# Grouped attention of a four-block network: each head's scores, transposes and projection products in two halves in place of four quarters

## The reference, cut to what matters

```
def _L1_attn_ref(x, Wq, Wk, Wv, Wo):          # x: 2 x 512 x 512
    q = einsum('bth,oh->bto', x, Wq)          # 32 heads x 128
    k = einsum('bth,oh->bto', x, Wk)          # 8 heads x 128
    v = einsum('bth,oh->bto', x, Wv)          # 8 heads x 128
    q = q * cos + _rotate_half(q) * sin
    k = k * cos + _rotate_half(k) * sin
    qg = q.reshape(B, 8, 4, T, 128)
    scores = einsum('bkgtd,bksd->bkgts', qg, k) / sqrt(128)
    scores = where(causal, scores, -inf)
    attn = softmax(scores, axis=-1)
    out = einsum('bkgts,bksd->bkgtd', attn, v)
    return einsum('bto,ho->bth', out, Wo)
```

## Time and profile before

| | us |
|---|---|
| median of 3 runs | 2234.25 (2228.36 to 2234.79) |
| the profiled execution's own time | 2234.35 |
| its span in the profile | 2232.6 |
| TensorE busy (matrix products) | 2007.4, 90% of the span |
| TensorE weight loads busy | 1263.8, 57% |
| VectorE busy | 1110.2, 50% |
| ScalarE busy | 777.2, 35% |
| GpSimd busy | 742.5, 33% |

### The profile page before, as it was taken

How to read it: one execution, slowest core, us unless ns; L and a number is a source line. 1 busy time by engine, 2 the same in 40 slices (tenths; PEclk the granted TensorE clock), 3 DMA queues, 4 the chain that set the end, 5 groups by cost and what they waited for, 6 DMA issues and landing times.

```text
span 2232.6 us, 28279 instructions
## 1 busy us (share of the span) xinstructions
PE 2007.4 (90%) x10566; PEld 1263.8 (57%) x10566; DVE 1110.2 (50%) x2019; ACT 777.2 (35%) x1649; POOL 742.5 (33%) x1199
## 2 busy tenths in 40 slices
PE   5899866999999999999998897979999788998887
PEld 2444432777777777777775685844444444544333
DVE  3656445555555555555555414135556335565344
ACT  0455523333332333333332232313565302564311
POOL 1444402534343334443332343412444202343200
PEclk9899977999999999999999897989999989999999
DMA  7222100101010101010000421134333006111100
GB/s 185 33 42 38 62 19 1 48 1 48 1 48 1 48 1 48 1 48 22 27 29 1 166 101 52 54 42 46 58 59 101 11 0 72 31 42 39 42 19 19
DMA packets 45337, 95.02 MB, mean 43 GB/s; under 512 B 7593, under 2 KB 35625, under 8 KB 41897
## 3 DMA queue, kind: packets, MB, share of 16 engines
q1 hardware_dynamic: 45202, 93.22, 16.7%
HBM read 62.20 MB, written 2.10 MB: 29 GB/s over the span
## 4 chain that ended last, share of the span: by engine, by line
PE 80%; DVE 9%; issue 4%; ACT 3%; DMA 2%; POOL 1%; SPq 1%; POOLq 0%; ACTq 0%; DVEq 0%
PE PS L1259 10%; PE PS L1328 8%; PE PS L1311 6%; PE PS L1284 6%; PE PS L535 6%; PE PS L1663 5%; PE PS L432 5%; PE PS L513 4%; PE PS L479 4%; PE PS L560 4%; PE PS L1296 3%; PE PS L1270 3%; PE PS L1674 3%; PE PS L1639 2%; PE PS L447 2%
## 5 line engine op out<-in xcount | busy, mean ns | idle before, releaser
L937 ACT ACTIVATE PB<-PS 128x512 f32<-128x512 f32 x480 | 279.4, 600 | 238.7 <-PE PS L513 235.0
L721 DVE TENSOR_REDUCE NM<-PS 128x2 f32<-128x1024 f32 x192 | 209.1, 1091 | 230.9 <-PE PS L481 229.6
L844 POOL TENSOR_SCALAR_AFFINE_SELECT PB<-PB 128x256 f32<-128x256 f32 (+1 forms) x480 | 172.7, 366 | 342.3 <-ACT PB L937 336.9
L1457 ACT COPY PRT<-PS 128x512 f32<-128x512 f32 (+3 forms) x256 | 108.8, 425 | 415.5 <-PE PS L1296 410.9
L479 PE MATMUL PS<-KQ 96*128 96x512 bf16 (+3 forms) x768 | 188.3, 310 | 30.3 <-DMA KQ<-LOW 15.9
L1417 DVE TENSOR_REDUCE NX<-PS 128x1 f32<-128x512 f32 (+3 forms) x256 | 124.1, 490 | 169.9 <-PE PS L1285 168.0
L1576 POOL TENSOR_SCALAR PR<-PR,RCP 128x512 f32<-128x512 f32 (+3 forms) x256 | 135.6, 535 | 199.7 <-DVE RCP L1405 193.4
L513 PE MATMUL PS<-KQ 99*128 99x512 bf16 (+3 forms) x768 | 184.0, 306 | 7.6 <-ACT PB L937 3.4
L1284 PE MATMUL PS<-kT,qT 128*128 128x512 f32 (+3 forms) x512 | 183.6, 440 | 4.2 <-ACT PR L1523 4.0
L432 PE MATMUL PS<-XTT,WA 128*128 128x512 f32 x288 | 149.6, 630 | 22.1 <-DMA XTT<-xT 19.3
L274 POOL TENSOR_TENSOR rstd<-ve,halfneg 128x1 f32<-128x1 f32 x64 | 44.1, 689 | 369.3 <-DVE ve L250 369.3
(11 more groups left out here) (257 smaller groups left out, 4043.5 us busy)
## 6 DMA issues: line engine op xcount, KB each, us to landing
KQ<-HI SPq DMA_DIRECT2D x108, 128.0 KB, 3.9
KQ<-MID SPq DMA_DIRECT2D x72, 128.0 KB, 4.7
WB<-f_w SPq DMA_DIRECT2D x12, 768.0 KB, 4.3
WB<-w1o SPq DMA_DIRECT2D x8, 1024.0 KB, 7.9
WC<-f_w SPq DMA_DIRECT2D x10, 768.0 KB, 4.5
WB<-w1a SPq DMA_DIRECT2D x8, 768.0 KB, 4.4
WB<-w1b SPq DMA_DIRECT2D x8, 768.0 KB, 5.9
WA<-w SPq DMA_DIRECT2D x6, 1024.0 KB, 7.6
```

The source lines that it names most:

```text
L721: x = dve.tensor_reduce(nm[:, h:h + 2, i], PS[:, b:b + 2, 0:(i + 1) * P], AX.X, ALU.max, negate=True)
L844: pool.affine_select(blocks, blocks, [[0, count], [1, P]], ALU.is_ge, 0.0, base=0, channel_multiplier=-1).then_inc(s16["probs_ready"].sem, 1)
L937: act.activation(PB[:, n % PBS, :], PS[:, 4 + n % 2, :], ACT.Exp, scale=self.scale)\
```

## The change

In each head the loop over four quarters becomes a loop over two halves. In a half, TensorE first gets both blocks' scores, then both blocks' transposes of the head before, then two steps of the projection. The instructions are the same, and so are all waits in them. The DVE, ACT, POOL and SP queues are not touched.

```
-                    for i in range(NT):
-                        self.scores(pe, n, i)
-                        if n:
-                            self.transpose_probs(pe, n - 1, i)
-                        next(q, None)
+                    for half in ((0, 1), (2, 3)):
+                        for i in half:
+                            self.scores(pe, n, i)
+                        for i in half:
+                            if n:
+                                self.transpose_probs(pe, n - 1, i)
+                        for i in half:
+                            next(q, None)
```

## The result

The changed kernel takes 2259.52 us (median of 4 runs, 2259.18 to 2260.38), the kernel before 2231.33 on the same occasion (2228.36 to 2234.79). The ratio is 1.0126, 95% interval 1.0106 to 1.0146: 28 us slower. The forecast was 2261, worked out as 26.7 us more.

What follows compares the result with a forecast made beforehand. The prediction took TensorE, busy for 90% of the span, as the bound. Waits of 25.1 us in heads 1 to 61, 1.6 in heads 62 and 63 and 0 for TensorE's own work, added to 2234.35, gave 2261; range 2251 to 2272.

Steps and rivals of the forecast that it cites:

- TensorE's own work: nothing: Moving scores and transposes on TensorE costs 0 us in itself, between a gain of 10 and a loss of 7.
- Scores 2: no new wait: Two projection steps just cover exponential 0, with scores 2 ready at 3.69 us and TensorE there at 3.79; h = 1, 2 unchanged.
- Scores 3 wait 0.36 or 0.46: Scores 3 wait for exponential 1: 0.36 us for h = 0 and 3, 0.46 for h = 1 and 2; 25.1 us in all.
- Nothing gives it back: After scores 3 in each head, no later wait shrinks, and DVE's rotation and the next row maximum keep their place.
- The other signs: On ACT, exponential 0 of h = 0 starts 0.4 us later against the head's start, and copy 1 follows without a gap.
- Heads 62 and 63: +1.6: The last two heads, without projection steps, already wait for ACT and lose 1.2 and 0.4 us more.
- the gain from fewer changes of work: Rival: first products after transposes, 475 against 392 ns, become fewer on TensorE, saving 10 us; 3% for a faster kernel.
- The rival that ACT's order hides the wait: Scores 3 would find exponential 1 done, so no change, 2234 to 2238 us; chance 4%.
- The clock rival: Seven transposes in a row and a gap per head drop TensorE to 1.2 GHz: 51 us more, 2312; chance 2%.

Runs made afterwards that it cites:

- copy 1 moved: The changed kernel with one step of ACT's queue moved, copy 1 behind exponential 1 instead of ahead of it; 2237.54 us, ratio 1.0020 to the kernel before.
- first half grouped: The changed kernel with each head's second half put back to quarters, so only blocks 0 and 1 are grouped; 2229.27 us, ratio 0.9985 to the kernel before.
- the step between scores 2 and 3: The changed kernel with one of the second half's two projection steps put between scores 2 and scores 3; 2267.59 us, ratio 1.0148 to the kernel before.
- ACT in halves: The changed kernel with ACT's queue in halves, two exponentials and then two copies in each; 2253.43 us, ratio 1.0091 to the kernel before.
- the full change with the DVE moves: The changed kernel with the copy of the values and the next key's rotation moved later on DVE; 2254.40 us, ratio 1.0093 to the kernel before.

## Why the prediction was right

The time came out 1.5 us from the forecast. That it is so close is in part luck: the forecast started from 2234.35 us, where the median of the kernel before is 2231.33, and added 26.7, where the medians lie 28.2 apart, so two errors cancel. In the profiled executions the growth is 25.4 us, and there the end of the stage gave 2.1 us more than forecast, heads 0 and 1 0.8 less, and parts that the change does not touch another 2.5 less. What was not luck is the sum over heads 2 to 61. Step by step:

- *TensorE's own work: nothing.* Half right. Seven transposes cost 0.77 and a projection step 0.70, as said. But 0.10 us a head of h = 0 or 3 are lost to weight loads behind masks, shown by the run with copy 1 moved. In the full change only the 0.05 of scores 1 can show, since scores 3 wait anyway, and only where no wait takes it in: with the first half grouped it cost 1.8 us in all, in the 30 heads of h = 0 and 3, and nothing for h = 1 and 2. The Trainium skill's rate for weight loads (TensorE: Matmul & The Clock Gate, section LDWEIGHTS) had given an estimate of 0.05 us a head, 3 us in all. The trace agrees with the 0.05 (scores 1 take 0.70 in place of 0.65) but with 3 us no better than with my 0.
- *Scores 2: no new wait.* Right for h = 0 and 3 (in the first half grouped they take 0.43, in the same position). That they wait "as long as before, to the hundredth" for h = 1 and 2 is wrong, to the good side: with the first half grouped they show 0.49 and 0.65 in place of 0.54 and 0.70, because TensorE comes to them 0.05 us later, and in the full change, for h = 1, their weight load starts 0.10 us ahead of them (721.42, 721.52), where before it started beside them.
- *Scores 3 wait 0.36 or 0.46.* The mechanism is right and the sizes nearly so: heads grew by 0.40 for h = 0 and 3, the 0.36 plus most of the load of scores 1. For h = 2 they grew by 0.45 (0.46 forecast). For h = 1 the rows put exponential 0 at 2.79 us of the head, for DVE's sake. It is still DVE that sets it, but the row maximum ends 0.05 us earlier against the head's start (2.65 in place of 2.70), the exponential starts at 2.74, and the head grows by 0.39. Sum over heads 2 to 61: 24.6, where 60 heads by the forecast give 24.6 too. That these agree so well is again in part luck: the errors in h = 0 and 3 (1.2 us too little) and in h = 1 (1.1 too much) cancel.
- *Nothing gives it back.* Right: the growth is the same in every unit but one, to 0.02 us. The other signs came too: exponential 0 of a head with h = 0 starts 2.63 us after the head in place of 2.19, and copy 1 follows it without a gap.
- *Heads 62 and 63: +1.6.* Too small. Head 62 itself went as said, 6.36 us from scores 0 to the product (6.33 forecast). But the product then took 4.10 us where it had taken 2.41, which is the clock (below), and head 63 took 8.21 us up to its product where it had taken 7.47 (7.89 forecast), also with a clock below 1.00 in part. Together +3.7. (What starts at 1207.83 is ACT's exponential, behind DVE's row maximum.)

Of the rivals, the gain from fewer changes of work is refuted: the first product after transposes is still listed as longer, and grouping alone (first half) gains nothing in the heads. The rival that ACT's order hides the wait is refuted by the 61 new places in the table. The clock rival is refuted inside the stage, where the granted clock is 1.00 from 430 to 1180 us with seven transposes in a row in each head. At the stage's end the clock did cost some 2 us, which the forecast did not have.

## What to carry to other kernels

Where an engine is full and its partner's queue is strictly in order, the two orders are one schedule: regrouping one without the other turns work that covered a wait into work that stands behind it. Before such a change, write the partner's queue beside the new order with its measured lengths, and follow it to the next two places that wait; a cover put back at the first place (the step between scores 2 and 3) or a partner's queue turned round wholesale (ACT in halves) mostly just moved the wait. And look in a tight kernel for the third engine's work that stands ahead of what the full engine waits for: moving 2.8 us of DVE work a unit to an idle place gave more than any order of TensorE tried here.

## What the runs showed of the hardware

At the stage's end TensorE waits often, and its granted clock there differs between the kernels. The product with the values in head 62, by stretch, before and after (columns as in the earlier trace rows). Before:

```profile
1201.30:1203.70 2.40, 2.40 (x9) 1.60 (x10) 0.16 (x1) 0.19 (x2) 0.82 (x2) 1.00 0.00 0
```

After:

```profile
1224.70:1228.80 4.10, 4.10 (x9) 2.39 (x10) 0.16 (x1) 0.21 (x2) 0.84 (x2) 0.58 0.02 4
```

In the first the clock is at its upper level of 2.4 GHz, in the second for most of the time at the lower of 1.2, after a head in which TensorE was busy for 4.12 of 6.40 us, against 4.14 of 5.20 before. With the first half grouped, the whole end ran at the upper level:

```profile
1195.60:1224.00 28.40, 18.83 (x97) 12.06 (x95) 16.05 (x40) 10.89 (x32) 6.95 (x12) 1.00 0.00 1
```

There the end took 28.4 us, against 31.5 before, where the stretch 1211.2 to 1227.5 had a mean granted clock of 0.74.

Two things speak for the clock as what moves these times. The first is the runs. With the first half grouped, nine of ten lie between 2228.14 and 2230.58 us, with a mean granted clock of 0.950 over the whole execution; the tenth took 2237.21 at 0.946. The runs of the kernel before fall near 2228 or near 2234 on one and the same occasion: of nine, six took 2228.11 to 2229.43 us at 0.948 to 0.950, three 2233.89 to 2234.43 at 0.947. An estimate from the stretches: the end of the stage at 0.84 in place of 1.00 for 31.5 us lowers the mean over 2232 us by 0.002, most of what lies between 0.947 and 0.950.

The second is what went before in head 62. By the starts in TensorE's order of time (up to 0.17 us ahead of the chain's), four profiled executions took longest from scores 0 to the product (6.1 to 6.5 us: the full change, the step between scores 2 and 3, copy 1 moved, the full change with the DVE moves). In these, the time from that product's start to the next scores was 3.6 to 3.9 us. In the other six, with 5.3 to 6.0 us, it was 2.23 in each. So the order of TensorE and ACT seems to have a part in it. This rests on one execution of each kernel, and no run changed the waits of head 62 alone; that they cause it is not shown.
